# Output projection of an attention block: weights stationary instead of head outputs, three split products of 512 columns, result transposed back

## What is computed

```python
mod = (silu(c) @ wmod).reshape(8, 6, 1, 256)
sa, ca, ga, sb, cb, gb = (mod[:, i] for i in range(6))
ga = (2 * (ga >= 0) - 1) * maximum(abs(ga), 0.25)       # gb likewise
h = layernorm(x) * (1 + ca) + sa
qkv = h @ W_pack                                        # 16 query heads, 8 key and 8 value heads of 128
probs = softmax(where(mask, q @ k.T / sqrt(128), min))
out = (probs @ v).reshape(b, s, 16 * 128)
x = x + ga * (out @ W_o)                                # W_o is 2048 x 256: the output projection
h = layernorm(x) * (1 + cb) + sb
x = x + gb * ffn(h)
```

## Time and profile before

| | |
|---|---|
| median of 3 runs | 774.26 us (773.07 to 779.81) |
| profiled execution, first to last instruction (span) | 772.5 us |
| PE busy / weight load busy | 742.1 us (96%) / 618.5 us (80%) |
| DVE, ACT, POOL busy | 538.4, 441.9, 423.9 us |
| TensorE clock granted, mean | 0.995 of full |

### The profile page before, as it was taken

How to read it: one execution, slowest core, us unless ns; L and a number is a source line. 1 busy time by engine, 2 the same in 40 slices (tenths; PEclk the granted TensorE clock), 3 DMA queues, 4 the chain that set the end, 5 groups by cost and what they waited for, 6 DMA issues and landing times.

```text
span 772.5 us, 12283 instructions
## 1 busy us (share of the span) xinstructions
PE 742.1 (96%) x3858; PEld 618.5 (80%) x3858; DVE 538.4 (70%) x1676; ACT 441.9 (57%) x1145; POOL 423.9 (55%) x337
## 2 busy tenths in 40 slices
PE   3899999999999999999999999999998999999997
PEld 2688778888888888878888887888886767777775
DVE  3598777689877777987777798787856214464375
ACT  4687767676876567587756767785645222222110
POOL 0553344555465478845537884653634536578356
PEclk9999999999999999999999999999999999999999
DMA  8960005800003201100220100231329679996772
GB/s 296 317 137 1 2 1 162 297 0 1 1 1 111 81 32 48 39 9 1 96 70 32 47 33 2 76 112 53 119 65 283 221 224 304 290 257 77 161 234 82
DMA packets 62351, 84.45 MB, mean 109 GB/s; under 512 B 6312, under 2 KB 50229, under 8 KB 62288
## 3 DMA queue, kind: packets, MB, share of 16 engines
q1 hardware_dynamic: 51440, 70.56, 29.2%
q0 software_dynamic: 7680, 8.95, 6.0%
q10 hardware_dynamic: 3168, 4.17, 1.6%
HBM read 54.88 MB, written 33.51 MB: 114 GB/s over the span
## 4 chain that ended last, share of the span: by engine, by line
PE 83%; DVE 8%; SPq 3%; ACT 2%; DMA 1%; issue 1%; ACTq 0%
PE PJ L1303 23%; PE OUT L1407 12%; PE U L1396 6%; PE U L1356 6%; PE U L1557 5%; PE U L1385 5%; PE U L1503 3%; PE U L1397 3%; PE U L1355 3%; PE OUT L1503 3%; PE U L1303 3%; PE OUT L1576 2%; PE XB L1576 2%; PE XB L1303 2%; DMA xin<-in_dram 1%; PE XB L1379 1%
## 5 line engine op out<-in xcount | busy, mean ns | idle before, releaser
L747 POOL TENSOR_TENSOR qsw<-qsw,sinT 128x512 f32<-128x512 f32 x96 | 124.0, 1291 | 215.7 <-ACT qsw L528 215.0
L541 ACT ACTIVATE U<-U,nmax 128x128 f32<-128x128 f32 (+1 forms) x256 | 98.9, 386 | 79.6 <-DVE nmax L956 79.4
L956 DVE CUSTOM_DVE_ANT_0 U<-U,mask 128x128 f32<-128x128 f32 (+1 forms) x256 | 86.7, 379 | 74.6 <-PE U L1356 74.4
L1407 PE MATMUL OUT<-wo,oT 128*128 128x256 f32 x512 | 131.5, 380 | 0.0
L1303 PE MATMUL PJ<-hT_hi,w_hi 128*128 128x512 f32 x256 | 112.8, 441 | 4.6 <-DVE hT_lo L930 4.1
L1303 PE MATMUL PJ<-hT_lo,w_hi 128*128 128x512 f32 x256 | 101.7, 397 | 0.0
L1303 PE MATMUL PJ<-hT_hi,w_lo 128*128 128x512 f32 x256 | 101.5, 397 | 0.0
L966 DVE TENSOR_SCALAR prob<-U,rinv 128x128 f32<-128x128 f32 (+1 forms) x256 | 95.1, 413 | 4.5
L527 ACT ACTIVATE qsw<-PJ 64x512 f32<-64x512 f32 x96 | 56.9, 593 | 65.4 <-PE PJ L1303 60.0
L751 POOL TENSOR_TENSOR qr<-qr,qsw 128x512 f32<-128x512 f32 x64 | 82.9, 1295 | 19.6 <-DVE qr L944 15.9
L1407 PEld LDWEIGHTS OUT<-wo,oT 128*128 128x128 f32 x512 | 87.6, 191 | 6.6
(11 more groups left out here) (205 smaller groups left out, 1559.8 us busy)
## 6 DMA issues: line engine op xcount, KB each, us to landing
wgu<-in_dram SPq DMA_DIRECT2D x32, 352.0 KB
expert_sum<-blank SPq DMA_DIRECT2D x3, 2176.0 KB, 17.2
slot_rows<-blank SPq DMA_DIRECT2D x1, 4624.0 KB, 26.7
late_sums<-expert_sum SPq DMA_DIRECT2D x9, 512.0 KB, 9.7
wd_a<-in_dram SPq DMA_DIRECT2D x12, 352.0 KB
wraw<-in_dram SPq DMA_DIRECT2D x8, 512.0 KB, 12.3
bcm<-mod_rows SPq DMA_DIRECT2D x8, 512.0 KB, 6.8
xe<-slot_rows ACTq DMA_DIRECT2D x10, 289.0 KB
```

What stands on the lines that cost most here:

```text
L541: last = act.activation(U[n % 3][:, a:z], U[n % 3][:, a:z], ACT.Exp, scale=-1.0, bias=nmax[:, n % 4, j:j + 1], accum_out=rsum[:, n % 4, j: ...
L747: pool.tensor_tensor(pair3(qsw[:, n % NQSW, :]), pair3(qsw[:, n % NQSW, :]), both(sinT[:, :]), ALU.mult).then_inc(t2_done, 1)
L956: last = dve.tensor_tensor_reduce(out=U[n % 3][:, a:z], in0=U[n % 3][:, a:z], in1=mask[:, a:z], scale=-float(HD) ** -0.5, scalar=3.4e38, o ...
L1407: last = pe.matmul(OUT[b][:, t * H:(t + 1) * H], oT[:, n % NOT, t * PN:(t + 1) * PN], wo[:, head, :], start=(head == 0 and t == 0), stop=( ...
```

## The change

The output projection is turned round. `wo` is split into `wo_hi` and `wo_lo` (in the first pair, four parts each, on ACT and DVE). The head output is split too: ACT writes `oT_hi` (`head_high`), DVE writes the rest `oT_lo` (`head_low`). Once both sequences of a head are there, PE keeps 128 x 128 of the split `wo` standing and streams 512 columns, both sequences, in three products into `OUT[c]`, where c is the half of the 256 output features. One half of a head is done per step, and the last one comes one step later than before. The result stands with features on partitions, so the gate is a per-partition scalar (`gateT`), and PE transposes the gated result back (`post_x1`, eight transposes for a pair), which DVE adds to the residual instead of POOL. The hooks behind it move to later steps (tables of `l`), and at the end `gate_up(0, 2)` moves ahead of the last output products. Also: the probabilities are normalised by one DVE instruction instead of two, the mask table is 256 columns instead of 384, the broadcast rows lose the first gate.

```diff
+            def head_high(n):
+
+                act.wait_ge(pv_ps, n + 1)
+                act.activation(oT_hi[:, (n // 2) % 2, n % 2, :], U[n % 3][:, 0:S], ACT.Copy).then_inc(ot_hi_done, 1)
+
+            def wo_high(j):
+
+                if j == 0:
+                    act.wait_ge(ld_wo, 16)
+                h = slice(j * WO_PART, (j + 1) * WO_PART)
+                act.activation(wo_hi[:, h, :], wo[:, h, :], ACT.Copy).then_inc(wo_hi_done, 1)
...
+                if 0 <= n - 2 < NU:
+                    head_high(n - 2)
                 if 0 <= n < NU:
                     exps_of(n)
...
-            def head_out(n):
-                dve.wait_ge(pv_ps, n + 1)
-                dve.tensor_copy(oT[:, n % NOT, :], U[n % 3][:, 0:S]).then_inc(ot_done, 1)
+            def head_low(n):
+
+                dve.wait_ge(ot_hi_done, n + 1)
+                dve.tensor_tensor(oT_lo[:, (n // 2) % 2, n % 2, :], U[n % 3][:, 0:S],
+                                  oT_hi[:, (n // 2) % 2, n % 2, :].bitcast(F32), ALU.subtract).then_inc(ot_done, 1)
...
-                for j, (a, z) in enumerate(((0, PN), (PN, 3 * PN))):
-                    last = dve.tensor_scalar(prob[:, n % 2, a:z], U[n % 3][:, a:z], rinv[:, n % 4, j:j + 1], None, ALU.mult)
-                last.then_inc(norm_done, 1)
...
+                dve.tensor_tensor(prob[:, n % 2, :].rearrange("p (j k) -> p j k", k=PN),
+                                  U[n % 3][:, 0:3 * PN].rearrange("p (j k) -> p j k", k=PN),
+                                  rinv[:, n % 4, 1:4].unsqueeze(2).broadcast_to([PN, 3, PN]), ALU.mult).then_inc(norm_done, 1)
...
+            def post_gate(p, c):
+
+                dve.wait_ge(y_ps, 2 * p + (c + 1))
+                if p == 0 and c == 0:
+                    dve.wait_ge(gate_done, 1)
+                for b in range(2):
+                    last = dve.tensor_scalar(yT[:, c, b, :], OUT[c][:, b * S:(b + 1) * S], gateT[:, c, 2 * p + b:2 * p + b + 1],
+                                             None, ALU.mult)
+                last.then_inc(yt_done, 1)
...
-                    if l in (1, 2):
-                        post_gate(p, l - 1)
-                    if l == 4:
+                    if l in (3, 4):
+                        post_gate(p, l - 3)
+                    if l in (5, 6):
+                        post_x1(p, l - 5)
+                    if l == 8:
                         post_stats(p, 0)
                         post_stats(p, 1)
-                    if l in (6, 7):
-                        post_h2(p, l - 6)
...
-                for t in range(2):
-                    last = pe.matmul(OUT[b][:, t * H:(t + 1) * H], oT[:, n % NOT, t * PN:(t + 1) * PN], wo[:, head, :],
-                                     start=(head == 0 and t == 0), stop=(head == NH - 1), skip_group_check=True)
+                for i, (w, o) in enumerate(((wo_hi, o_hi), (wo_lo, o_hi), (wo_hi, o_lo))):
+                    last = pe.matmul(y, w[:, head, cols], o, start=(head == 0 and i == 0), stop=(head == NH - 1 and i == 2),
+                                     skip_group_check=True)
...
-                if 0 <= n - 3 < NU:
-                    output(n - 3)
+                if n >= LEAD:
+                    output((n - LEAD) // 2, n % 2)
...
+                if n == NU + 1:
+                    gate_up(0, 2)
...
-            gate_up(0, 2)
             pe.wait_ge(ot_done, NU)
-            for f in range(3, FT):
+            gate_up(0, 3)
+            for b in range(2):
+                post_x1(LAST, b)
+            for f in range(4, FT):
                 gate_up(0, f)
```

More of the change, by code:

```diff
@@ L222, in adaln_block, with x1_bank @@
         DN = (OUT[1], U[2])
+        def x1_bank(p, b):
+            return OUT[b] if p == LAST else XB
         def xnt_bank(p, b):
@@ L330, in next_step @@
             return p + 1, l
-        STEPS = range(-LEAD, NU + 3)
+        STEPS = range(-LEAD, NU + 4)
         block = ctx.enter_context(nc.Block())
@@ L572, in post_squares @@
                 for t in range(2 * b, 2 * b + 2):
-                    last = act.activation(yg[:, b, t % 2, :], h2[:, t, :], ACT.Square, accum_out=rms[:, 0, t:t + 1])
+                    last = act.activation(yT[:, b, t % 2, :], h2[:, t, :], ACT.Square, accum_out=rms[:, 0, t:t + 1])
                 own(last)
@@ L601, in hooks @@
                     prepare_norm(q)
-                if l == 5 and p >= 0:
+                if l == 9 and p >= 0:
                     post_std(p, 0, 2)
@@ L635, in mod_rows @@
                 act.wait_ge(mod_ps, j + 1)
-                act.activation(mod[:, j * 2 * H:(j + 1) * 2 * H], XB[0:B, :], ACT.Copy).then_inc(rows_done, 1)
+                if j == 0:
+                    act.activation(mod[:, 0:2 * H], XB[0:B, :], ACT.Copy).then_inc(rows_done, 1)
+                else:
+                    act.activation(gateT[:, :, :], XB[:, H:H + HC * B].rearrange("p (c b) -> p c b", b=B), ACT.Copy)
+                    act.activation(mod[:, 2 * H:3 * H], XB[0:B, 0:H], ACT.Copy).then_inc(rows_done, 1)
             act.wait_ge(ld_const, 128)
@@ L783, in _ @@
             while c < TT * TOPK:
-                for _ in range(2 if at % 4 == 3 and at % UNITS not in (3, 15, 19) else 1):
+                for _ in range(2 if at % 4 == 3 and at % UNITS not in (19, 23) else 1):
                     if c < TT * TOPK:
@@ L1075, in post_slots @@
                 dve.wait_ge(pos_used, p + 1)
-                own(dve.tensor_tensor(key[:, :, :], key[:, :, :], kept[:, :, :], ALU.mult))
+                own(dve.tensor_tensor(key[:, :, :], key[:, :, :], zz2[:, :, 0:E], ALU.mult))
             def post_keys(p):
@@ L1472, in mod_rows @@
             def mod_rows(j):
-                pe.wait_ge(ld_wmr, 16)
-                for c in range(HC):
-                    last = pe.matmul(XB[0:B, :], scT[:, c, :], wm[:, c, 2 * H + j * 2 * H:2 * H + (j + 1) * 2 * H],
-                                     start=(c == 0), stop=(c == HC - 1))
+                if j == 0:
+                    pe.wait_ge(ld_wmr, 16)
+                    for c in range(HC):
+                        last = pe.matmul(XB[0:B, :], scT[:, c, :], wm[:, c, 3 * H:5 * H], start=(c == 0), stop=(c == HC - 1))
+                else:
+                    for c in range(HC):
+                        pe.matmul(XB[0:B, 0:H], scT[:, c, :], wm[:, c, 5 * H:6 * H], start=(c == 0), stop=(c == HC - 1))
+                    for k in range(HC):
+                        at = H + k * B
+                        for c in range(HC):
+                            last = pe.matmul(XB[:, at:at + B], wm[:, c, 2 * H + k * PN:2 * H + (k + 1) * PN], scT[:, c, :],
+                                             start=(c == 0), stop=(c == HC - 1))
                 last.then_inc(mod_ps, 1)
```

240 lines of the change are left out of this document (129 added, 111 removed).

## The result

The changed kernel takes 779.91 us (median of 12 runs, 776.74 to 784.03), the kernel before 774.35 us (12 runs, 772.97 to 781.97). The ratio is 1.0068, with a 95% interval of 1.0043 to 1.0092: 0.7% slower. The ratios in this document are estimated over all fast runs and so differ a little from the quotient of two medians (here 1.0072). The forecast was 765.8 us with a range of 756 to 779. The profiled execution has a span of 776.8 us (its time is 779.01 us), 4.3 us over the 772.5 us of before.

A forecast was written before the change was run, and what follows sets the result against it. PE was taken as the bound, DVE not far behind. The terms -22.4 + 2.6 - 2.9 + 3.5 + 2.5 + 8.2 gave -8.5 us, so 774.3 became 765.8 us, range 756 to 779.

The forecast's parts named there:

- Price of the products: Output projection on PE: three split products take 0.70 us instead of 0.87, no format-switch cost taken; 22.4 us less.
- First pair: Splitting four `wo` parts on ACT and DVE between the packed weights' parts: +3.5 us, of 0 to 8.
- with the slack above I count nothing for that: Transposes back in the pairs wait for DVE's gate one or two steps earlier; 1.4 us slack, so no cost.
- I expect the DVE losses ... to fall to 1.5: Inside pairs 2 to 4: PE's waits on DVE, some 8 us, fall to 1.5 as DVE is relieved.
- ACT's burst: Steps l = 10 to 15: ACT's bunched hooks exceed the slack, 1.2 us per pair, 3.6 in three.
- Last steps before T: Before the last unit's values product ends: router and slot hooks move to steps without packed projection, +2.5 us, of 0 to 4.
- T to the transposes: From the end of the last unit's values product to the `xn` transposes: 22.5 us instead of 14.3, +8.2 us.
- Everything behind hangs on these transposes and keeps its length: All work after the transposes of `xn` near the end: shifts with them, no change in length.
- ACT as the bound in every step: Rival, attention steps: ACT's in-order waits for values product and row maximum set the pace; 784 us, chance 0.08.
- Upper ends, 772 us: Rival: format switches cost 0.03 us per group (+4), pairs and first pair lose 2 us more; chance 0.19.
- PE's idle time between T and the transposes: Sign of being right: PE idle about 9 us from the last unit's values product to the transposes of `xn`.

The follow-up runs named there:

- e1_gate: Changed kernel with DVE's gate hooks moved early, to l = 2 and 3 ahead of the step's other hooks: 776.68 us, ratio 1.0016 to the kernel before.
- e11_rope: Changed kernel with POOL's rotary multiplication by the sines left out, the addition kept: 772.74 us, ratio 0.9988 to the kernel before.
- e7_norm: Kernel before the change, with only the normalising of probabilities done by one DVE instruction instead of two: 774.04 us, ratio 1.0006.
- e2: Changed kernel with POOL's last scatters of pair 3 released in twos by the shared products: 774.98 us, ratio 1.0009 to the kernel before.
- e5: Changed kernel with gate hooks early, POOL's scatters released in twos, end reordered and input split's hooks later: 764.40 us, ratio 0.9881 to the kernel before.
- e6: Changed kernel with gate hooks early, end reordered and input split's hooks later, POOL's old scatter waits kept: 766.95 us, ratio 0.9910 to the kernel before.

## Why the prediction was wrong

The profiled executions are 12.8 us further apart than forecast (+4.3 instead of -8.5): 5.6 of it up to T, 0.6 from T to the transposes of `xn`, 4.7 from there to the first expert, 1.9 in the last shared products.

**Price of the products: right.** 0.69 us per group, router products 131.9 us apart where some 131 were forecast, no cost of changing formats.

**First pair: right in the sum by luck, the term 1.9 us too small.** +3.5 us was forecast; the first scores of pair 2 come 2.1 us earlier, as 5.6 - 3.5 has it. But 1.9 of that lie ahead of the first scores of the first pair. The pair itself is 0.2 us shorter where the products save 5.6, so splitting `wo` there costs 5.4 us in this execution, inside the bounds of 0 to 8.

**"with the slack above I count nothing for that": the step that failed first.** I held the wait for the gate to be one of the transposes back, with one or two steps in hand. The wait that matters is another: the first output product of the next pair waits for the same gate, now with no step in hand, behind other work on DVE. It cost 1.2 us in each of pairs 2 and 3 and 0.3 in pair 4; e1_gate gives it back.

**"I expect the DVE losses ... to fall to 1.5": wrong.** The losses of before were 1.2, 2.9 and 2.0 us in pairs 2, 3 and 4 by the lengths of the steps (6.1 in all, where "some 8" was read from the router distance of pair 3), on l = 8 and 9, in pairs 3 and 4 also on l = 3, in pair 3 on l = 7. They did go, but others came, in pair 2 larger ones: of 131.8 - 128.5 = 3.3 us in pair 2, 1.2 are the gate, 1.0 DVE on l = 17 to 20, 0.5 ACT on l = 14 and 15; 0.6 are spread. In pair 4, l = 11 to 14 lose 1.9 us where the kernel before lost nothing; e11_rope halves that. DVE's part comes from POOL holding it, which the earlier trace rows showed me (2.65 us) and which I took to be over with POOL's residual addition. POOL's rotary work is enough. ACT's burst, which I put at 1.2 us per pair, costs 0.5. e7_norm shows that DVE's average load, on which I had built the relief, is hardly what counts.

**Last steps before T: not shown by themselves.** The gap at T (5.6 us by the table) is 3.1 us in each of pairs 2 and 3, and pair 4 with the last steps even gains 0.6 more than the 3.4 forecast. The low clocks have their part in this: 1.6 of pair 3's 3.1 us, and 1.6 of what pair 4 seems to gain. Without them pair 4 and the last steps are 1.0 us worse than forecast.

**T to the transposes: right.** T + 23.1 against T + 22.5, by the chain as I wrote it.

**"Everything behind hangs on these transposes and keeps its length": wrong, 4.7 us.** It doesn't keep its length, since POOL's scatters of pair 3 (thirteen left instead of eight) are released by the shared products, which moved: `post_base` slid into DVE's router chain, PE's pause grew to over 3 us, and PE came out of it at half its clock. The hold is shown by e2, e5 and e6, where it goes with POOL's release. The clock is shown by the fourteen traces together: it is low behind the six pauses of 3.4 to 3.5 us ahead of the prefix and full in the eight traces with less than 1 us of pause there or none. The +1.9 us of the last stretch is the same kind of meeting, but nine of eleven traces of the changed kernel and its edits don't have it: there the forecast of no change was right, and the profiled execution was unlucky.

**The rivals.** ACT as the bound in every step is refuted (steps without hooks take 3.73 us). "Upper ends, 772 us" had the right kind, ACT and DVE bunches, but not the size and not the place behind T. The range, to 779, ended just short of 779.91. PE's idle time between T and the transposes, forecast as about 9 us, is 8.3: 3.4 up to 572, 3.5 up to 580, 1.4 ahead of the transposes.

## What to carry to other kernels

When a hook moves, list who waits for its result in the next round of the loop, not only who uses it next: a buffer that is written over is a wait, too. When the bound engine gets faster, price the work of the others by its place: a saving on PE is worth its length only on steps where nobody else has a hook. And behind a point that comes later, nothing "keeps its length" that is released by something which moved otherwise, POOL's queue above all.

## What the hardware showed that I had not expected

A DVE instruction with two inputs in SBUF, or `tensor_scalar` from SBUF to SBUF, that starts beside a running POOL tensor operation is not done before that one ends: 0.23 becomes 1.24 us (the floor), 0.20 becomes 1.28 (the carry, of 32 columns), 0.29 becomes 1.42, and 128x1024 goes from 1.2 to 3.4. `MAX8`, `MATCH_REPLACE8` and `TENSOR_REDUCE` ran beside POOL at their usual length (0.49 for four, 0.18 and 0.28 us), as did those that read one of two operands from PSUM (`prob` took 0.56 us in each of its 64 instances in pairs 2 and 3). That is what the Trainium skill (SBUF — State Buffer, Who interferes with whom) states: DVE and GpSimd share one pair of ports, taken for a whole instruction by whoever comes first, and a DVE instruction with at most one SBUF input outside the two-port modes stays clear of it. The trace agrees, and I should have applied it to the earlier trace rows.

PE's granted clock also fell where PE had been busy without a break: behind the router hook of pair 3, with PE busy 4.00 of 4.00 us, in the changed kernel:

```profile
396.00:400.00 4.00, 4.00 (x28) 3.72 (x28) 1.81 (x6) 0.49 (x2) 1.44 (x2) 0.87 0.63 223
400.00:404.00 4.00, 4.00 (x17) 3.28 (x16) 1.39 (x6) 2.25 (x7) 1.28 (x1) 0.70 0.00 1
```

It comes in some executions and not in others (in e11_rope the stretch is at full clock), and before the change it shows at 524 to 532 us. The fourteen traces have 42 router hooks inside the pairs. At 17 of them the clock fell within about 1 us of the end of the 24 router products (34 columns each, some 0.11 us apart), and nowhere else between 45 and 555 us. Such a fall costs the two steps there some 1.6 us. It is part of the spread of all these kernels: the twelve runs of the changed kernel go from 776.74 us at a mean clock of 0.991 to 784.03 at 0.983. Why it falls behind some router hooks and not behind others stays open.
